# A routed 3x3 convolution whose taps are laid out as half-width matrix products, five pairs of them in place of six full-width ones

## The chip, the cores and the metric

The kernel runs on one core of a Trainium2 chip. Its time is the device time of one launch in microseconds (us), and the time of a kernel is the median of its runs. The engines of the core work side by side and are ordered by semaphores alone: TensorE (PE in the profile; PEld is its weight load), VectorE (DVE), ScalarE (ACT), GpSimd (POOL), and SyncE (SP), which issues most of the DMAs.

## The reference

The input is 32 images of 32x32 pixels and 64 channels, float32. Two stages follow one another, each on a group norm of its input and each added to its input. The first, in which the change lies, is cut to this:

```python
def routed_conv(x, q, Wk, Wv, Wmlp, alpha, We, be):      # x: (32, 32, 32, 64)
    allowed = ones((32, 4))
    for t in range(3):
        k, v = x @ Wk, x @ Wv                             # two heads of 16
        attn = softmax(einsum("nd,bsnd->bns", q, k) / 4)  # over the 1024 pixels
        pooled = einsum("bns,bsnd->bnd", attn, v)
        logits = pooled.reshape(32, 32) @ Wmlp
        weights = softmax(where(allowed, logits, -1e9) / 1.5)
        wsel = weights kept for the two best of four experts, normed to 1
        x_mod = x * (1 + attn.mean(heads) * 1024 * softplus(alpha))
        x = sum_e wsel[:, e] * (conv3x3(x_mod, We[e]) + be[e])
        allowed = allowed without the best expert (the last one stays)
    return x
```

The second stage is two selective state space passes (Mamba), over the rows and over the columns of each image.

## The kernel before

**Layout.** An image lies in 128 partitions by 512 columns: partition 64 r + c holds channel c of the image's rows of parity r (0 the even rows, 1 the odd ones), 16 rows of 32 pixels each. Since a convolution is linear in its weights, the four experts' weights are mixed for each image first, and one 3x3 convolution is made with the mixed weights.

**The convolution.** An output row of one parity needs its own row and the rows above and below it. In this layout three matmuls of 128x128 weights with the padded image `padded` (`pad` in the rows), shifted by the column offset dx = 0, 1, 2, give two of the three row taps for both parities (`conv_main`). What is missing is the tap that lies a whole row pair away: the row above for parity 0, which is a parity 1 row of the pair before, and the row below for parity 1. It takes `shifted` (`shf`), a copy of `padded` moved by one row pair, and three more 128x128 matmuls, of whose weights only the two anti-diagonal 64x64 blocks are not zero (`conv_anti`). Mixed weights `w_mixed` (`wm`) have 2 x 3 x 128 = 768 columns.

**Phases.** The images go in 4 bodies of 8: two groups of 4 (`TEAM`), whose three steps alternate, so that a body has 6 phases, `k` = 0 to 5, and the kernel 24, `P` = 6 i + k. Every engine runs its own written-out program, a `slot` for each phase. In the slot of phase P, the attention and routing of P are worked out, while TensorE makes the convolutions of phase P - 1, which belong to the other group. The order on each engine is that of the code, and is fixed:

- TensorE: `conv_main` of image 0, score of image 3, `conv_anti` of image 0, swap (the largest score over both parities), `conv_main` 1, total (sums of the softmax), `conv_anti` 1, logits, modulation (`p_modul`, the attention map), `conv_main` and `conv_anti` of images 2 and 3, and the scores of images 0 to 2 of the next phase.
- ScalarE: the exponential of the scores (the line that writes `attn_map` from `p_route`; called **the exponential** below), copies of the convolutions' results to `xc`, the exponential of the logits, the map (`attn_map` from `p_modul`), the first product of the mix for the images (`mix`), in some phases the group norm's scaling, and at the end `shift` for the images 0 to 3, which writes `shf`. The next slot begins with the next exponential.
- VectorE: the largest score (`top`), the mixing of weights (three operations for each image, `mix` and `wm`), and the chain of small operations on sums, logits and ranks.
- SyncE stores the map to `map_scratch` and loads it back, spread over the partitions, as `map_all`. GpSimd multiplies `map_all` by `xc` into `pad`, image by image.

So a phase is a ring: the exponential, sums, map, out and back by DMA, `pad`, `shift`, the next exponential. What `shift` waits for stands ahead of it:

```python
        ge(act, conv_done, 4 * (P - 2) + a + 1)
        act.wait_ge(padded_ready, 4 * P + a + 1)
```

Phases differ in what is added. In k = 1 to 4 the results are copied by ScalarE; in k = 5 and 0 VectorE adds the last step's results to the input instead (`step_last`). A group norm is applied in the slots k = 5 and 0 (of the next inputs), and k = 1 and 2 of all bodies but the first (of the outputs). The second stage begins as the last convolutions run, with the first image of the first body.

Of the kernel before, what the change touches and what calls it, by code (L numbers as in the profile page):

```python
# [22 lines left out]
UNITS = IMAGES * 4  # L23
MAIN, ANTI = 3 * 128, 3 * 64
PHASES = 2 * STEPS
# [4 lines left out]
def build(nc, x_in, wk, q, wvT, wmlp, alpha, we, be, mamba_w, out, mid_x, mid_n):  # L30
# [5 lines left out]
    def sb(name, shape, dt=f32):  # L36
        return ctx.enter_context(nc.sbuf_tensor(name, shape, dt))
# [4 lines left out]
    with ctx:  # L42
# [15 lines left out]
        gain = sb("gain", [128, 4])  # L58
        we_sb = sb("we_sb", [128, EXPERTS, 2 * MAIN])
        be_sb = sb("be_sb", [128, EXPERTS])  # L60
# [44 lines left out]

        def anti_of(rows, half, e):
            return we_sb[rows, e, MAIN:].rearrange("p (d c) -> p d c", d=3)[:, :, 64 * half:64 * half + 64]

        first_loads = [(wk_sb[:], wk), (q_sb[:], q.partition_broadcast(128)), (wv_sb[:], wvT), (wmlp_sb[:], wmlp),
                       (gain[:, 0:1], alpha.partition_broadcast(128))]  # L110
        expert_loads = [(be_sb[:], be), (we_sb[:, :, 0:MAIN], we[:, :, 0:MAIN])]
        for par in range(2):
            rows = slice(64 * par, 64 * par + 64)
            for e in range(EXPERTS):
                expert_loads.append((anti_of(rows, 1 - par, e), we[rows, e, MAIN:].rearrange("p (d c) -> p d c", d=3)))
        mamba_loads = []
# [120 lines left out]
        def _(dve):  # L237
# [7 lines left out]
            nc.vector.memset(route[:], 0.0).then_inc(dve_chain, 1)  # L245
            for e in range(EXPERTS):
                for par in range(2):
                    nc.vector.memset(anti_of(slice(64 * par, 64 * par + 64), par, e), 0.0)
            s1["norm_first"](dve)
# [82 lines left out]
def stage1(nc, ctx, memory, x_in, mid_x, norm_rows, c):  # L332
# [6 lines left out]
    R = TEAM * 4 * HEADS * 2  # L339
    ZEROS, ZEROS_DVE = 2 * TEAM * 3, 2 * TEAM * 2 + 2  # L340
    def sb(name, shape, dt=f32):
# [10 lines left out]
    for g in two:  # L352
        xc.append([sb(f"xc_{g}{a}", [128, PIX]) for a in team])
        padded.append([sb(f"pad_{g}{a}", [128, ROWS2, SIDE + 2]) for a in team])
        shifted.append([sb(f"shf_{g}{a}", [128, ROWS2, SIDE + 2]) for a in team])
        w_mixed.append([sb(f"wm_{g}{a}", [128, 2, 3, 128]) for a in team])
        if g == 0:
            mix0 = [sb(f"mix0_{b}", [128, 768]) for b in two]
            map_all = sb("map_all", [128, TEAM, PIX])
            attn_map = sb("attn_map", [128, PIX])  # L360
            attn, map_rows = attn_map[0:R, :], attn_map[R:R + 2 * TEAM, :]
            scrap = sb("scrap", [R, PIX])
            mod_w = sb("mod_w", [R, 128])
    for g in two:
# [177 lines left out]
    def conv_main(pe, i, k, a):  # L542

        g, P = k % 2, i * PHASES + k
        bank = p_conv[a]
        pe.wait_ge(w_ready, 4 * P + a + 1)
        pe.wait_ge(padded_ready, 4 * P + a + 1)

        if k:
            conv_taken(pe, i, k - 1, a)  # L550
        elif i:
            conv_taken(pe, i - 1, PHASES - 1, a)
        elif a == 0:
            pe.wait_ge(c["mamba_ready"], 1)
        for dx in range(3):
            nc.tensor.matmul(bank[:], w_mixed[g][a][:, 0, dx, :], padded[g][a][:, :, dx:dx + SIDE],  # L556
                             start=(dx == 0), stop=False)

    def conv_anti(pe, i, k, a):

        g, P = k % 2, i * PHASES + k
        bank = p_conv[a]
        pe.wait_ge(shifted_ready, 4 * P + a + 1)
        for dx in range(3):
            mm = nc.tensor.matmul(bank[:], w_mixed[g][a][:, 1, dx, :], shifted[g][a][:, :, dx:dx + SIDE],  # L565
                                  start=False, stop=(dx == 2))
        mm.then_inc(conv_done, 1)
# [13 lines left out]
    def tensor_program(pe, prepare):  # L581
        def score(i, k, a):
# [7 lines left out]
            else:  # L590
                pe.wait_ge(x_step, 16 * i + (4 * (k - 2) + a + 1))
            mm = nc.tensor.matmul(p_route[:], route[:, 128 * a:128 * a + 128], xc[g][a][:], start=(a == 0), stop=(a == TEAM - 1))
            if a == TEAM - 1:
# [82 lines left out]
    def shift(act, P, g, a):  # L676

        ge(act, conv_done, 4 * (P - 2) + a + 1)
        act.wait_ge(padded_ready, 4 * P + a + 1)
        nc.scalar.copy(shifted[g][a][0:64, 0:ROWS2 - 1, :], padded[g][a][0:64, 1:, :])  # L680
        nc.scalar.copy(shifted[g][a][64:128, 1:ROWS2, :],  # L681
                       padded[g][a][64:128, :ROWS2 - 1, :]).then_inc(shifted_ready, 1)

# [155 lines left out]
    def mix_last(dve, P, g, a):  # L839
        dve.wait_ge(mix_ready, 8 * P + (3, 4, 7, 8)[a])  # L840

        ge(dve, conv_done, 4 * (P - 2) + a + 1)
        nc.vector.scalar_tensor_tensor(w_mixed[g][a][:].rearrange("p m d c -> p (m d c)"), c["we"][:, 3, :],  # L843
                                       wsel[:, a, 3:4], mix0[a % 2][:], ALU.mult, ALU.add).then_inc(w_ready, 1)

    def norm_first(dve):
# [6 lines left out]
        norm_scale(dve, 0)  # L853
        for g in two:
            for a in team:
                nc.vector.memset(shifted[g][a][0:64, ROWS2 - 1, :], 0.0).then_inc(zeroed_dve, 1)
                nc.vector.memset(shifted[g][a][64:128, 0, :], 0.0).then_inc(zeroed_dve, 1)

# [854 lines left out]
```

## Time and profile before

| | us |
|---|---|
| median of 3 runs | 3948.51 (3946.25 to 3951.95) |
| profiled execution, its own time | 3952.92 |
| its span in the trace | 3951.1 |
| first exponential of the first stage | at 27.5 |
| 24th exponential | at 644.1 |
| VectorE busy over the span | 3750.3 (95%) |
| TensorE | 3655.9 (93%) |
| GpSimd | 3278.0 (83%) |
| ScalarE | 2937.1 (74%) |

The busy shares are over the whole span, five sixths of which is the second stage. What bounds the first stage is read from its own stretch and from the order of the instructions in one phase. A matmul on float32 data stands in the trace as two instructions, one for each of two passes, so that "x6" is three matmuls of the code.

### The profile page before, as it was taken

What the parts mean: (1) busy time and instruction counts of PE and PEld (TensorE: products, weight loads), DVE (VectorE), ACT (ScalarE), POOL (GpSimd) and SP (SyncE); (2) the same over time, 40 slices, a digit from 0 to 9 for tenths busy, and PEclk for the clock granted to TensorE, in tenths of its full rate; (3) what the DMA queues carried; (4) which work ended last, traced back from release to release, by engine and by line L of the source; (5) the groups of instructions that cost most, each with busy time, mean ns of one, the idle gap of its engine ahead of it and who ended that gap; (6) DMA issues with size and microseconds to landing.
All of it is one profiled execution on the core that took longest, in us unless ns stands there. A gap on an engine that the chain in (4) does not pass through costs nothing. (4 is left out here: it accounts for less than half of the span.)

```text
span 3951.1 us, 34661 instructions
## 1 busy us (share of the span) xinstructions
PE 3655.9 (93%) x8780; PEld 1520.5 (38%) x8780; DVE 3750.3 (95%) x3409; ACT 2937.1 (74%) x4422; POOL 3278.0 (83%) x1542
## 2 busy tenths in 40 slices
PE   7999999899999999999999999999999999999998
PEld 3444444333333333333333333333333333333333
DVE  7778787999999999999999999999999999999998
ACT  3454554788777788888888878888888888887785
POOL 2221222899999999999999999999999999999998
PEclk9999999999999999999999999999999999999999
DMA  4142324888889888988889988899888898998886
GB/s 113 33 130 57 108 73 151 322 341 341 340 344 353 344 342 348 349 346 338 347 347 344 352 352 345 343 351 347 347 339 346 346 346 347 352 351 340 343 345 254
DMA packets 203159, 1181.08 MB, mean 299 GB/s; under 512 B 30960, under 2 KB 31760, under 8 KB 68816
## 3 DMA queue, kind: packets, MB, share of 16 engines
q1 hardware_dynamic: 200128, 1177.64, 78.3%
q10 hardware_dynamic: 2832, 1.23, 0.1%
q8 instruction: 70, 1.15, 0.1%
q14 instruction: 129, 1.06, 0.1%
HBM read 1144.03 MB, written 34.73 MB: 298 GB/s over the span
## 5 line engine op out<-in xcount | busy, mean ns | idle before, releaser
L1547 POOL TENSOR_TENSOR read<-state,bc_all 128x1024 f32<-128x1024 f32 x1024 | 2399.4, 2360 | 127.6 <-DVE state L1611 97.7
L1611 DVE TENSOR_TENSOR_SCAN state<-decays,p_drive 128x1024 f32<-128x1024 f32 x1024 | 2297.8, 2274 | 35.2 <-ACT p_drive L1446 12.2
L1316 PE MATMUL p_y<-read,ident 128*128 128x512 f32 x4096 | 1920.5, 602 | 12.8 <-POOL read L1547 12.8
L1438 ACT ACTIVATE decays<-dt,wa 128x496 f32<-128x496 f32 x2048 | 1337.1, 703 | 122.1 <-DVE state L1611 119.7
L1316 PEld LDWEIGHTS p_y<-read,ident 128*128 128x128 f32 x4096 | 766.2, 191 | 987.6 <-issue 841.8
L1598 DVE TENSOR_TENSOR p_drive<-bc_all,p_dtx 128x1024 f32<-128x1024 f32 x768 | 906.3, 1210 | 0.0
L1564 POOL TENSOR_TENSOR pool_drive<-dtx,bc_all 128x1024 f32<-128x1024 f32 x256 | 602.4, 2353 | 4.4 <-DMA bc_all<-bc_scratch 4.2
L766 POOL TENSOR_TENSOR pad<-map_all,xc 128x512 f32<-128x512 f32 x96 | 139.5, 1483 | 519.1 <-DMA map_all<-map_scratch 455.3
L1446 ACT COPY p_drive<-pool_drive 128x1024 f32<-128x1024 f32 x256 | 260.8, 1019 | 271.5 <-DVE state L1611 271.5
L1312 PE MATMUL p_y<-xconv,d_diag 128*128 128x512 f32 x256 | 145.1, 649 | 204.2 <-DVE gated L1621 204.2
L556 PE MATMUL p_conv<-pad,wm 128*128 128x512 f32 x576 | 267.6, 600 | 1.2 <-issue 0.8
L565 PE MATMUL p_conv<-shf,wm 128*128 128x512 f32 x576 | 265.5, 597 | 1.3 <-ACT shf L681 1.3
L1554 POOL TENSOR_TENSOR dtx<-dt,xconv 128x512 f32<-128x512 f32 x128 | 163.6, 1278 | 12.0 <-ACT dt L1410 12.0
L705 ACT ACTIVATE mix<-we_sb,wsel 128x768 f32<-128x768 f32 x96 | 87.1, 933 | 116.2 <-DVE wm L843 72.4
L1292 PE MATMUL p_b<-soft,ident 128*128 128x512 f32 x256 | 144.4, 646 | 30.0 <-ACT soft L1431 30.0
L1394 ACT ACTIVATE gate<-p_b 128x512 f32<-128x512 f32 x128 | 76.4, 597 | 120.7 <-PE p_b L1269 66.2
L1387 ACT ACT_TABLE_LOAD x128 | 164.2, 1283 | 2.3
L1398 ACT ACT_TABLE_LOAD x128 | 164.2, 1283 | 2.3
L1312 PEld LDWEIGHTS p_y<-xconv,d_diag 128*128 128x128 f32 x256 | 38.3, 188 | 310.3 <-DVE gated L1621 309.3
L556 PEld LDWEIGHTS p_conv<-pad,wm 128*128 128x128 f32 x576 | 104.8, 189 | 136.2 <-issue 115.3
L565 PEld LDWEIGHTS p_conv<-shf,wm 128*128 128x128 f32 x576 | 106.6, 189 | 130.0 <-issue 122.9
L1255 PE MATMUL p_a<-cols_in,w_cols 128*128 128x256 f32 x640 | 148.8, 378 | 1.0 <-issue 0.5
(162 smaller groups left out, 3215.7 us busy)
## 6 DMA issues: line engine op xcount, KB each, us to landing
bc_all<-bc_scratch SPq DMA_DIRECT2D x1024, 1024.0 KB, 7.2
map_all<-map_scratch SPq DMA_DIRECT2D x48, 512.0 KB, 5.7
norm_rows<-xn SPq DMA_DIRECT2D x32, 280.0 KB, 5.6
norm_in<-norm_rows SPq DMA_DIRECT2D x64, 140.0 KB, 8.1
norm_in<-norm_rows SPq DMA_DIRECT2D x64, 139.8 KB, 8.3
fresh<-in_x SPq DMA_DIRECT2D x32, 256.0 KB, 6.6
x<-in_x SPq DMA_DIRECT2D x32, 256.0 KB, 3.5
mid_x<-x SPq DMA_DIRECT2D x32, 256.0 KB, 6.5
```

Of the source, the lines that this page charges most:

```text
L556: nc.tensor.matmul(bank[:], w_mixed[g][a][:, 0, dx, :], padded[g][a][:, :, dx:dx + SIDE], start=(dx == 0), stop=False)
L565: mm = nc.tensor.matmul(bank[:], w_mixed[g][a][:, 1, dx, :], shifted[g][a][:, :, dx:dx + SIDE], start=False, stop=(dx == 2))
L1312: nc.tensor.matmul(p_y[:], d_diag[unit[0]][:], xconv[b][:], start=True, stop=False).then_inc(skip_added, 1)
L1316: nc.tensor.matmul(p_y[:], ident[:], read[:, s % DEEP, :], start=False, stop=(s == N - 1)).then_inc(y_added, 1)
L1387: nc.scalar.activation(same_shape(xconv[b][:], m), in_order(p_a, m), ACT.Silu, bias=wcb[m][:]).then_inc(xconv_ready, 1)
L1398: nc.scalar.preload_act_table_set("natural_log_exp_and_others")
L1438: nc.scalar.activation(decays[:, s % DEEP, :].rearrange("p (q t) -> p q t", t=SIDE)[:, :, 1:], dt[b][:, :, 1:], ACT.Exp, scale=wa[m][:, s: ...
L1446: nc.scalar.copy(p_drive[:, s % 4:s % 4 + 2, :], pool_drive[n][:]).then_inc(drive_moved, 1)
L1547: nc.gpsimd.tensor_tensor(read[:, s % DEEP:s % DEEP + 2, :], state[:, s % DEEP:s % DEEP + 2, :], bc_all[s // CHUNK][:, :, 1, :], ALU.mult) ...
L1564: nc.gpsimd.tensor_tensor(pool_drive[n][:], dtx[b][:].unsqueeze(1).broadcast_to([128, 2, PIX]), bc_all[s // CHUNK][:, :, 0, :], ALU.mult). ...
L1598: nc.vector.tensor_tensor(p_drive[:, 2 * (p % 2):2 * (p % 2) + 2, :], bc_all[p][:, :, 0, :], p_dtx[:].unsqueeze(1).broadcast_to([128, 2, P ...
L1611: nc.vector.tensor_tensor_scan(state[:, at:at + 2, :].rearrange("p s n -> p (s n)"), decays[:, at:at + 2, :].rearrange("p s n -> p (s n)") ...
```

## The change

The two anti-diagonal blocks of `conv_anti` are not put into a 128x128 matrix with zeros. Each parity's output gets products of its own, with 64 columns of weights (all 128 partitions of input), and writes its own half of the bank's partitions. `conv_main` is three pairs of such products. For the taps that are missing, three of 64 channels for each parity, two of them share one product's 128 partitions of input and the third has one for itself, so that `conv_anti` is two pairs. Each parity therefore has a `shifted` buffer of its own, which holds the missing rows twice: once as they were, and once, in the other 64 partitions, one column further. `shift` makes four copies an image in place of two. The `shifted` buffers are no longer doubled over the two groups, so that `shift` waits for the convolution of the phase before (`P - 1`) and not for the one before that. Mixed weights have 384 + 256 = 640 columns in place of 768. The scores are split into two half-width products as well. Expert loads, zeroed regions and the placing of buffers follow.

```diff
-MAIN, ANTI = 3 * 128, 3 * 64
+MAIN, ANTI = 3 * 128, 4 * 64
+MIX = MAIN + ANTI
...
         for dx in range(3):
-            nc.tensor.matmul(bank[:], w_mixed[g][a][:, 0, dx, :], padded[g][a][:, :, dx:dx + SIDE],
-                             start=(dx == 0), stop=False)
+            for par in two:
+                nc.tensor.matmul(bank[CH * par:CH * par + CH, :],
+                                 w_mixed[g][a][:, 128 * dx + CH * par:128 * dx + CH * par + CH],
+                                 padded[g][a][:, :, dx:dx + SIDE], start=(dx == 0), stop=False)
...
-        for dx in range(3):
-            mm = nc.tensor.matmul(bank[:], w_mixed[g][a][:, 1, dx, :], shifted[g][a][:, :, dx:dx + SIDE],
-                                  start=False, stop=(dx == 2))
+        for n in two:
+            for par in two:
+                at = MAIN + 128 * par + CH * n
+                mm = nc.tensor.matmul(bank[CH * par:CH * par + CH, :], w_mixed[g][a][:, at:at + CH],
+                                      shifted[par][a][:, :, 1 + n:1 + n + SIDE], start=False, stop=(n == 1))
...
-            mm = nc.tensor.matmul(p_route[:], route[:, 128 * a:128 * a + 128], xc[g][a][:], start=(a == 0), stop=(a == TEAM - 1))
+            for part in two:
+                mm = nc.tensor.matmul(p_route[R * part:R * part + R, :], route[:, 128 * a + R * part:128 * a + R * part + R],
+                                      xc[g][a][:], start=(a == 0), stop=(a == TEAM - 1))
...
-        ge(act, conv_done, 4 * (P - 2) + a + 1)
+        ge(act, conv_done, 4 * (P - 1) + a + 1)
         act.wait_ge(padded_ready, 4 * P + a + 1)
-        nc.scalar.copy(shifted[g][a][0:64, 0:ROWS2 - 1, :], padded[g][a][0:64, 1:, :])
-        nc.scalar.copy(shifted[g][a][64:128, 1:ROWS2, :],
-                       padded[g][a][64:128, :ROWS2 - 1, :]).then_inc(shifted_ready, 1)
+        for par, source, there, here in ((0, slice(64, 128), slice(1, ROWS2), slice(0, ROWS2 - 1)),
+                                         (1, slice(0, 64), slice(0, ROWS2 - 1), slice(1, ROWS2))):
+            crossed = slice(64 * par, 64 * par + 64)
+            nc.scalar.copy(shifted[par][a][source, there, 1:], padded[g][a][source, here, 1:])
+            o = nc.scalar.copy(shifted[par][a][crossed, there, 1:], padded[g][a][source, here, :SIDE + 1])
+        o.then_inc(shifted_ready, 1)
...
-        nc.vector.scalar_tensor_tensor(w_mixed[g][a][:].rearrange("p m d c -> p (m d c)"), c["we"][:, 3, :],
+        nc.vector.scalar_tensor_tensor(w_mixed[g][a][:], c["we"][:, 3, :],
                                        wsel[:, a, 3:4], mix0[a % 2][:], ALU.mult, ALU.add).then_inc(w_ready, 1)
```

On ScalarE, between the last results of one phase and the map of the next, there stood before (`xc` is the result of image 3, then come the copies of the four images, then the next slot's exponential):

```order
L698 ACTIVATE xc<-p_conv,bias 128x512
L680 COPY shf<-pad 64x510
L681 COPY shf<-pad 64x510
L680 COPY shf<-pad 64x510
L681 COPY shf<-pad 64x510
L680 COPY shf<-pad 64x510
L681 COPY shf<-pad 64x510
L680 COPY shf<-pad 64x510
L681 COPY shf<-pad 64x510
L714 ACTIVATE attn_map,parts<-p_route,neg_top 64x512
L698 ACTIVATE xc<-p_conv,bias 128x512
L721 ACTIVATE prob<-logit 128x16
```

Now sixteen copies stand in that place; these are the last two images' eight and what follows:

```order
L698 COPY shf<-pad 64x15x33
L699 COPY shf<-pad 64x15x33
L698 COPY shf<-pad 64x15x33
L699 COPY shf<-pad 64x15x33
L698 COPY shf<-pad 64x15x33
L699 COPY shf<-pad 64x15x33
L698 COPY shf<-pad 64x15x33
L699 COPY shf<-pad 64x15x33
L732 ACTIVATE attn_map,parts<-p_route,neg_top 64x512
L716 ACTIVATE xc<-p_conv,bias 128x512
L739 ACTIVATE prob<-logit 128x16
```

The exponential stands behind eight more copies than before, and each copy is of 495 elements in 15 pieces instead of 510 in one.

On TensorE a phase read as follows before, from its first convolution to the modulation and the next convolutions:

```order
L556 MATMUL p_conv<-pad,wm 128x512 x3
L592 MATMUL p_route<-xc,route 128x512
L565 MATMUL p_conv<-shf,wm 128x512 x3
L598 MATMUL p_small<-top,neg_swap 128x1
L556 MATMUL p_conv<-pad,wm 128x512 x3
L602 MATMUL p_small<-parts,both_par 128x2
L565 MATMUL p_conv<-shf,wm 128x512 x3
L606 MATMUL p_small<-ratios,ones 128x16
L612 MATMUL p_modul<-attn_map,mod_w 128x512
L556 MATMUL p_conv<-pad,wm 128x512 x3
L565 MATMUL p_conv<-shf,wm 128x512 x3
```

Now the same place reads:

```order
L566 MATMUL p_conv<-pad,wm 64x512 x6
L606 MATMUL p_route<-xc,route 64x512 x2
L578 MATMUL p_conv<-shf,wm 64x512 x4
L613 MATMUL p_small<-top,neg_swap 128x1
L566 MATMUL p_conv<-pad,wm 64x512 x6
L617 MATMUL p_small<-parts,both_par 128x2
L578 MATMUL p_conv<-shf,wm 64x512 x4
L621 MATMUL p_small<-ratios,ones 128x16
L627 MATMUL p_modul<-attn_map,mod_w 128x512
L566 MATMUL p_conv<-pad,wm 64x512 x6
L578 MATMUL p_conv<-shf,wm 64x512 x4
```

Here 64x512 is the size of a product's result. The order is the same; a full-width product of the convolution or the score has become a pair, and `conv_anti` has two pairs for three products. Three times in a phase a full-width product (swap; total; logits and modulation) stands between half-width ones.

## Rows read from the trace of the kernel before

**Rows 1.** Busy time by engine in a stretch of the first stage.

```profile
core 0: us, PE busy (x) PEld busy (x) DVE busy (x) ACT busy (x) POOL busy (x), PEclk, DMA share, GB/s
...
400.00:500.00 100.00, 100.00 (x254) 44.80 (x253) 75.22 (x203) 50.00 (x83) 16.31 (x14) 1.00 0.38 108
```

**Rows 2.** The exponential's line, all of its executions.

```profile
L714 ACT ACTIVATE attn_map<-p_route,neg_top x24: 682/682/682, 27.5 to 644.1; 64x512 f32<-64x512 f32 x24
```

**Rows 3.** Order of time (start us, us, what, count, [idle before <-releaser]): ScalarE, phase 15.

```profile
430.70 0.68 ACT L714 ACTIVATE attn_map<-p_route,neg_top 64x512 f32<-64x512 f32 x1 [1.73 <-DVE neg_top L916]
...
438.66 0.58 ACT L726 ACTIVATE attn_map<-p_modul 8x512 f32<-8x512 f32 x1
...
449.55 0.62 ACT L680 COPY shf<-pad 64x510 f32<-64x510 f32 x1 [0.39 <-POOL pad L766]
...
453.98 0.61 ACT L681 COPY shf<-pad 64x510 f32<-64x510 f32 x1
456.76 0.68 ACT L714 ACTIVATE attn_map<-p_route,neg_top 64x512 f32<-64x512 f32 x1 [2.17 <-DVE neg_top L916]
```

**Rows 4.** VectorE in order of time, phase 15: between exponential and map.

```profile
432.24 1.94 DVE L836 SCALAR_TENSOR_TENSOR mix<-we_sb,wsel,mix 128x768 f32<-128x768 f32 x2
...
435.89 0.28 DVE L946 TENSOR_SCALAR mod_w<-spread,kmap 64x128 f32<-64x128 f32 x1
436.09 1.00 DVE L843 SCALAR_TENSOR_TENSOR wm<-we_sb,wsel,mix 128x768 f32<-128x768 f32 x1
```

**Rows 5.** TensorE in order of time, phase 15: image 2, image 0 of the next slot.

```profile
437.28 2.84 PE L556 MATMUL p_conv<-pad,wm 128*128 128x512 f32 x6
...
450.26 2.74 PE L556 MATMUL p_conv<-pad,wm 128*128 128x512 f32 x6
```

**Rows 6.** GpSimd in order of time, phase 15: the four images' `pad`.

```profile
448.20 4.95 POOL L766 TENSOR_TENSOR pad<-map_all,xc 128x512 f32<-128x512 f32 x4 [20.85 <-DMA map_all<-map_scratch]
```

**Rows 7.** ScalarE in order of time, phase 14 (k = 2): exponential, first copy.

```profile
404.30 0.68 ACT L714 ACTIVATE attn_map<-p_route,neg_top 64x512 f32<-64x512 f32 x1 [1.63 <-DVE neg_top L916]
...
423.94 0.60 ACT L680 COPY shf<-pad 64x510 f32<-64x510 f32 x1
```

**Rows 8.** ScalarE in order of time, phase 5 (k = 5): exponential, first copy, next exponential.

```profile
159.28 0.68 ACT L714 ACTIVATE attn_map<-p_route,neg_top 64x512 f32<-64x512 f32 x1 [2.63 <-DVE neg_top L916]
...
181.44 0.60 ACT L680 COPY shf<-pad 64x510 f32<-64x510 f32 x1
...
187.50 0.68 ACT L714 ACTIVATE attn_map<-p_route,neg_top 64x512 f32<-64x512 f32 x1 [1.03 <-DVE neg_top L916]
```

**Rows 9.** VectorE in order of time, phase 5: last mix operations and step_last beside GpSimd.

```profile
176.60 3.97 DVE L843 SCALAR_TENSOR_TENSOR wm<-we_sb,wsel,mix 128x768 f32<-128x768 f32 x2
180.49 1.40 DVE L822 SCALAR_TENSOR_TENSOR x<-p_conv,bias,x 128x512 f32<-128x512 f32 x2
```

**Rows 10.** ScalarE, second stage: a 496-element operation in pieces.

```profile
685.73 2.50 ACT L1438 ACTIVATE decays<-dt,wa 128x496 f32<-128x496 f32 x4
```

**Rows 11.** TensorE, second stage: two half-width float32 products (x4), and their first two starts.

```profile
2059.43 0.67 PE L1335 MATMUL p_a<-gated,wo 128*64 128x256 f32 x4
...
2059.43 0.45 PE L1335 MATMUL p_a<-gated,wo 128*64 128x256 f32 x2
```

**Rows 12.** TensorE, second stage: one half-width product between full-width ones.

```profile
2006.82 1.45 PE L1316 MATMUL p_y<-read,ident 128*128 128x512 f32 x3
2008.20 1.07 PE L1325 MATMUL p_a<-gated,wo 128*64 128x512 f32 x2
2009.20 1.12 PE L1316 MATMUL p_y<-read,ident 128*128 128x512 f32 x2
```

**Rows 13.** Windows around a fall of TensorE's clock, second stage.

```profile
930.00:938.60 8.60, 6.46 (x15) 2.49 (x14) 8.60 (x7) 7.54 (x14) 7.97 (x5) 1.00 1.01 424
938.60:942.10 3.50, 3.50 (x5) 1.35 (x4) 3.41 (x3) 1.65 (x3) 3.42 (x2) 0.51 1.03 405
```

**Rows 14.** TensorE in order of time just before that fall.

```profile
938.22 1.72 PE L1312 MATMUL p_y<-xconv,d_diag 128*128 128x512 f32 x2 [1.90 <-DVE gated L1621]
```

**Rows 15.** VectorE: the last result of the first stage.

```profile
689.92 0.75 DVE L822 SCALAR_TENSOR_TENSOR x<-p_conv,bias,x 128x512 f32<-128x512 f32 x1 [2.17 <-PE p_conv L565]
```

More of the change, by code:

```diff
@@ L58, in build @@
         gain = sb("gain", [128, 4])
-        we_sb = sb("we_sb", [128, EXPERTS, 2 * MAIN])
+        we_sb = sb("we_sb", [128, EXPERTS, MIX])
         be_sb = sb("be_sb", [128, EXPERTS])
@@ L104, in build, with anti_of, tap_of @@
         dve_chain = sem("dve_chain")
-        def anti_of(rows, half, e):
-            return we_sb[rows, e, MAIN:].rearrange("p (d c) -> p d c", d=3)[:, :, 64 * half:64 * half + 64]
+        low, high = slice(0, 64), slice(64, 128)
+        def anti_of(rows, out_par, n):
+            at = MAIN + 128 * out_par + 64 * n
+            return we_sb[rows, :, at:at + 64]
+        def tap_of(rows, dx):
+            return we[rows, :, MAIN + 64 * dx:MAIN + 64 * dx + 64]
         first_loads = [(wk_sb[:], wk), (q_sb[:], q.partition_broadcast(128)), (wv_sb[:], wvT), (wmlp_sb[:], wmlp),
@@ L111, in build @@
         expert_loads = [(be_sb[:], be), (we_sb[:, :, 0:MAIN], we[:, :, 0:MAIN])]
[L112 to L115, printed above, removed]
+        for out_par, straight, crossed in ((0, high, low), (1, low, high)):
+            expert_loads += [(anti_of(straight, out_par, 0), tap_of(straight, 1)), (anti_of(straight, out_par, 1), tap_of(straight, 2)),
+                             (anti_of(crossed, out_par, 0), tap_of(straight, 0))]
         mamba_loads = []
@@ L245, in _ @@
             nc.vector.memset(route[:], 0.0).then_inc(dve_chain, 1)
-            for e in range(EXPERTS):
-                for par in range(2):
-                    nc.vector.memset(anti_of(slice(64 * par, 64 * par + 64), par, e), 0.0)
+            nc.vector.memset(anti_of(low, 0, 1), 0.0)
+            nc.vector.memset(anti_of(high, 1, 1), 0.0)
             s1["norm_first"](dve)
@@ L339, in stage1 @@
     R = TEAM * 4 * HEADS * 2
-    ZEROS, ZEROS_DVE = 2 * TEAM * 3, 2 * TEAM * 2 + 2
+    ZEROS, ZEROS_DVE = 2 * TEAM * 3, 2 * TEAM + 2
     def sb(name, shape, dt=f32):
@@ L354, in stage1 @@
         padded.append([sb(f"pad_{g}{a}", [128, ROWS2, SIDE + 2]) for a in team])
-        shifted.append([sb(f"shf_{g}{a}", [128, ROWS2, SIDE + 2]) for a in team])
-        w_mixed.append([sb(f"wm_{g}{a}", [128, 2, 3, 128]) for a in team])
+        w_mixed.append([sb(f"wm_{g}{a}", [128, MIX]) for a in team])
         if g == 0:
-            mix0 = [sb(f"mix0_{b}", [128, 768]) for b in two]
+            mix0 = [sb(f"mix0_{b}", [128, MIX]) for b in two]
+            scrap = sb("scrap", [R, PIX])
+            mod_w = sb("mod_w", [R, 128])
+            sb("spare", [128, 1760])
+            shf_00 = sb("shf_00", [128, ROWS2, SIDE + 2])
             map_all = sb("map_all", [128, TEAM, PIX])
@@ L361, in stage1 @@
             attn, map_rows = attn_map[0:R, :], attn_map[R:R + 2 * TEAM, :]
-            scrap = sb("scrap", [R, PIX])
-            mod_w = sb("mod_w", [R, 128])
+    for par in two:
+        shifted.append([shf_00 if a == par == 0 else sb(f"shf_{par}{a}", [128, ROWS2, SIDE + 2]) for a in team])
     for g in two:
@@ L563, in conv_anti @@
         pe.wait_ge(shifted_ready, 4 * P + a + 1)
-        for dx in range(3):
-            mm = nc.tensor.matmul(bank[:], w_mixed[g][a][:, 1, dx, :], shifted[g][a][:, :, dx:dx + SIDE],
-                                  start=False, stop=(dx == 2))
+        for n in two:
+            for par in two:
+                at = MAIN + 128 * par + CH * n
+                mm = nc.tensor.matmul(bank[CH * par:CH * par + CH, :], w_mixed[g][a][:, at:at + CH],
+                                      shifted[par][a][:, :, 1 + n:1 + n + SIDE], start=False, stop=(n == 1))
         mm.then_inc(conv_done, 1)
@@ L853, in norm_first @@
         norm_scale(dve, 0)
[L854 to L857, printed above, removed]
+        for a in team:
+            nc.vector.memset(shifted[0][a][:, 0, :], 0.0).then_inc(zeroed_dve, 1)
+            nc.vector.memset(shifted[1][a][:, ROWS2 - 1, :], 0.0).then_inc(zeroed_dve, 1)
     def last_vector(dve, part):
```

## The prediction

> **What bounds the kernel now.** I read the busy time by stretch first. In the first stage TensorE is busy all the time, the others half to three quarters [rows 1]. That suggests that fewer matmuls make it faster. But a phase is a ring, and one must see how close behind TensorE the ring's other parts are. So next I read one phase in order of time on each engine. The exponential is the best mark, since it comes once a phase: 24 of them from 27.5 to 644.1 us [rows 2], 26.8 us apart on average.
>
> In phase 15 they are 26.06 us apart [rows 3]. From the exponential to the first copy of `shift` pass 18.85 us: sums, `mod_w`, map, DMA out and back, `pad`. The eight copies start 0.633 us apart (7 steps from 449.55 to 453.98) and end at 454.59, 5.04 us after they began. Then ScalarE idles 2.17 us for `neg_top`, which hangs on TensorE [rows 3]. That 2.17 us is all the room the copies have. On TensorE, image 0 of the next slot starts at 450.26 [rows 5], 0.8 us after its `pad` is there (448.20 + 4.95/4 = 449.44) [rows 6]. So TensorE leads, but the ring through ScalarE and the DMAs is only 0.8 us (`pad`) and 2.2 us (`shift`) behind. Once TensorE is shortened by more than that, the ring decides.
>
> The 23 intervals between exponentials are of three kinds, counted in the same view. Eleven are as in phase 15 (ten at 26.1; the first one, with the preparations, 27.5). Six are as in phase 14, with a norm of outputs (26.3 to 26.4): 19.64 us to the first copy, then 6.76 [rows 3, 7]. Six are as in phase 5 (28.2; one is 29.3): 22.16 us to the first copy, then 6.06, and there the exponential already follows the end of the copies (181.44 + 5.03 = 186.47) by 1.03 us [rows 8]. Together 10 x 26.1 + 27.5 + 6 x 26.35 + 5 x 28.2 + 29.3 = 617, the 616.6 of [rows 2].
>
> **The change, part by part.**
>
> *TensorE's products.* From 437.28 to 450.26 stand 15 full products, four times three of the convolution and three scores: 0.865 us each, two passes of 0.43 [rows 5]. Do two half-width products run side by side? The second stage has such a pair, on 256 columns. Two passes end within 0.45 us, all four within 0.67 [rows 11], so the second pair of passes ends 0.22 after the first, where a lone pass of 256 columns would need 0.43/2 = 0.215. They run together, and a pair costs what one full product does: 0.43 to 0.44 a pass. Saved: 4 images x (6 - 5) = 4 products, 3.4 us a phase; the scores' pairs cost nothing.
>
> *Changing between full and half width.* In the second stage three full passes from 2006.82 would be followed at 2006.82 + 3 x 0.43 = 2008.11; the half-width product starts at 2008.20 (+0.09), holds the engine 1.00 in place of 0.86 (+0.14), and the next full product's two passes take 1.12 in place of the usual 1.02 (+0.10) [rows 12]. That is 0.34 us there and back, three times a phase: 1.0 us. TensorE's own need is then 26.06 - 3.4 + 1.0 = 23.7 us a phase.
>
> The Trainium skill has this in TensorEngine Tiling, Key Properties: a change of tiling mode drains the engine, while tiles of one mode work independently. The trace agrees with both, at 0.34 us and 0.22 us. By that page's table of theoretical speedup alone one would book the 3.4 us a phase and stop; that is the rival "hidden" below.
>
> *VectorE's mixing.* At 768 columns two operations take 1.94 us, one 1.00 [rows 4], a spacing of 0.94. At 512 columns two take 1.40 and one 0.75 [rows 9, 15], 0.65. For 640 I take 0.80, a gain of 0.14 each (bounds 0 and 0.16, the full proportion). Four stand between exponential and map: two `mix` at 432.24, one `wm` before `mod_w`, one before the logits that the map's line on ScalarE is queued behind [rows 3, 4]. The ring gains 0.55 us. In phases like 5 the first copy waits for ScalarE's last mix, which waits for `wm`. There four more `mix` (0.55), two `wm` that beside GpSimd take 1.99 each and should scale to 1.66 (0.65) [rows 9], and ScalarE's part (0.1) are won: 1.8 in all.
>
> *The copies.* Sixteen in place of eight, all ahead of the next exponential in ScalarE's queue. No row shows a copy of 64x15x33, or one from one half of the partitions to the other. Nearest above is the present copy, 0.633 for 510 elements [rows 3]. Nearest in size and in pieces are four operations of 496 elements in 2.50, under 0.625 each [rows 10]. Below, the map's line with 8 partitions still takes 0.58 [rows 3], so fewer partitions don't make it cheap. I take 0.61, with 0.58 and 0.66 as ends (the latter if pieces and crossing add 8% of the present copy). Sixteen take 9.8 us from first start to the exponential.
>
> *The new wait on the convolution of the phase before* costs nothing: image 3 of it is through before TensorE begins image 0 of the next slot, and that is after `pad` [rows 5, 6]. Loads, memsets and placement touch the start alone; I take zero.
>
> **The sum.** The new distance from first copy to next exponential is 9.8 us wherever the copies decide. `neg_top` comes earlier: TensorE needs, from `pad`, 3 + 1 + 2 pairs (5.2 us), swap and one change of width, about 6 us.
> - Like phase 15: 9.78 in place of 7.21 is +2.57, less 0.55: +2.0, eleven times, 22.2.
> - Like phase 14: 9.78 for 6.76 is +3.02, less 0.55, and less 0.2 since the first copy now follows `pad` directly (0.1 as in phase 15, not 0.3): +2.3, six times, 13.6.
> - Like phase 5: 9.78 for 6.06 is +3.72, less 1.8: +1.9, six times, 11.5.
>
> That is 47.3 us up to the 24th exponential. From there to the last result at 689.9 [rows 15] TensorE has 4 products fewer and a few more changes of width, and ScalarE has eight more copies among the second stage's first steps; they roughly cancel, +0.5. The second stage is untouched. 48 us on the profiled execution's own 3952.9 is 4001; the median before is 4.4 lower, so **3997**.
>
> Is TensorE really behind the ring then? From 437.28 to 450.26 it will have 13 pairs for 15 products: 11.2 us for 12.98, so image 0 waits some 0.7 us for `pad` (which moves little against `mod_w`). At total it has, from `pad`, 9 pairs, swap and changes, 8.2 us; the sums come at 0.1 + 9.8 + 1.5 (430.70 to 432.24) = 11.4 [rows 3, 4]. It idles 3.3 us there, every phase.
>
> **Rivals.**
>
> *The clock falls and TensorE leads again.* In the second stage, after an idle of 1.90 us, the granted clock is 0.51 for 3.5 us: the 1.2 GHz level [rows 13, 14]. A 3.3 us idle each phase invites it. Such a stretch costs up to 1.7 us of matmul time; about 1.0 us of it would fall into TensorE's wait for `mod_w` and 0.7 into the wait for `pad`, so one fall a phase costs nearly nothing, and two up to 1.7 x 23 = 39. I take +20 as this case: 4017. Dearer passes do the same: from 0.457 us a pass (13 pairs, 0.7 us of room) each 0.01 costs 0.26 a phase, 6 us in all. The skill's TensorE: Matmul & The Clock Gate, on HAM oscillation, warns of just such gaps between bursts; rows 13 show it here, and by the page alone one would expect it in each phase.
>
> *Halves do not overlap* in a long row of pairs, so the change doesn't do what its name says. Then 48 half products at 0.86, 2 and 1 us make 44.3 a phase: +18.2 x 24 = 437, 4385. Against it: rows 11, one pair long.
>
> *Faster: the copies stay hidden.* If the exponential did not wait for them, a phase like 15 would take 18.85 - 0.55 + about 5.9 = 24.2, near TensorE's 23.7: -1.9 x 24 = -45, 3904. It decides at a copy's spacing of (7.21 + 0.55)/16 = 0.48 us; every row of ScalarE at this size is at 0.58 or more.
>
> **Chances.** The sum as worked out 0.72, its own range 3984 to 4014 (copies -11 and +18 us, the rest +-3). Clock or passes 0.15. No overlap 0.03. Hidden 0.04. Cases between that and the sum 0.06, half of them within 0.2%, which is about what a measurement of this kernel can tell from no change. So faster 0.04, same 0.03, slower 0.93. The range of 8 in 10 reaches down a little below the sum's own and well into the clock's case: 3980 to 4030.
>
> **What would show it.** In the profile after: exponentials about 28 us apart in phases like 15, 28.6 like 14, 30 like 5; sixteen copies 0.61 apart ending right at the exponential, with ScalarE's idle before it gone; TensorE idle some 3 us before total, released by VectorE's sums, and no longer at full busy share; pairs of passes 0.43 apart with starts together. The prediction is wrong if the exponential does not follow the last copy, if copies cost under 0.5 or over 0.7, or if the granted clock of the first stage lies well under 0.9.

## The result, and the profile after

The changed kernel takes 4005.04 us (median of four, 4001.16 to 4008.35) against 3950.23 for the kernel before: a ratio of 1.0134, 95% interval 1.0115 to 1.0152. It is slower by 53 us going by the ratio, by 54.8 going by the two medians; the forecast was 3997, slower by 48. The profiled execution below is the fastest of the four, 4001.16 us on its own clock, 48.2 more than the profiled one before.

The exponential's line, all executions:

```profile
L732 ACT ACTIVATE attn_map<-p_route,neg_top x24: 682/682/683, 26.8 to 694.0; 64x512 f32<-64x512 f32 x24
```

From the first to the 24th pass 667.2 us, where it was 616.6 [rows 2]: 50.6 of the difference lies there. What comes after the 24th takes 3305.0 us of the span of 3999.0, before 3307.0. That is 2 us less, and the same part of the experiments' profiles differs by as much among themselves (3305.9 in the first, 3310.1 in the fifth below), so it says nothing.

ScalarE in phase 15, in order of time (start us, us, what, count, idle before and its releaser); between the shown copies stand fourteen more:

```profile
465.10 0.68 ACT L732 ACTIVATE attn_map<-p_route,neg_top 64x512 f32<-64x512 f32 x1
...
472.53 0.58 ACT L744 ACTIVATE attn_map<-p_modul 8x512 f32<-8x512 f32 x1
...
482.90 0.60 ACT L698 COPY shf<-pad 64x495 f32<-64x495 f32 x1 [0.87 <-POOL pad L784]
...
492.17 0.60 ACT L699 COPY shf<-pad 64x495 f32<-64x495 f32 x1
492.79 0.68 ACT L732 ACTIVATE attn_map<-p_route,neg_top 64x512 f32<-64x512 f32 x1
```

Set beside [rows 3], all three steps are there. The copies start (492.17 - 482.90)/15 = 0.618 us apart. The exponential begins 0.62 after the last one starts, and the idle time in brackets is gone: it waits for nothing but its queue. From first copy to exponential pass 9.89 us in place of 7.21. From exponential to map pass 7.43 in place of 7.96, the shorter mixing. No copy of the whole run waits for TensorE: where L698 has idle time before it (11 times, 8.5 us in all), `pad` ends it, and L699 never has any.

TensorE in the same phase:

```profile
462.40 2.80 PE L566 MATMUL p_conv<-pad,wm 128*64 128x512 f32 x12
466.78 0.38 PE L617 MATMUL p_small<-parts,both_par 128*128 128x2 f32 x2 [1.58 <-DVE parts L947]
467.09 1.94 PE L578 MATMUL p_conv<-shf,wm 128*64 128x512 f32 x8
...
470.23 1.12 PE L627 MATMUL p_modul<-attn_map,mod_w 64*128 64x512 f32 x2 [0.84 <-DVE mod_w L963]
```

Six half-width products, twelve passes, stand within 2.80 us, where three full ones take 2.84 us [rows 5]: pairs run side by side in a long row as well. And TensorE now waits twice, for the sums and for `mod_w`. The busy shares of a stretch show the same. TensorE has gone from 100.00 [rows 1] to 87.52, and the granted clock from 1.00 to 0.91:

```profile
core 0: us, PE busy (x) PEld busy (x) DVE busy (x) ACT busy (x) POOL busy (x), PEclk, DMA share, GB/s
400.00:500.00 100.00, 87.52 (x358) 29.55 (x358) 63.06 (x191) 65.82 (x113) 14.93 (x12) 0.91 0.35 108
```

Phase 2 shows what the clock does; its exponentials are 29.2 us apart, in phase 15 they are 27.7. First windows, then TensorE in order of time:

```profile
80.00:85.40 5.40, 3.04 (x15) 1.00 (x14) 0.92 (x4) 5.28 (x11) 0.00 (x0) 1.00 0.00 0
85.40:95.70 10.30, 9.51 (x22) 3.19 (x24) 8.28 (x30) 2.67 (x6) 0.00 (x0) 0.50 0.01 3
95.70:100.00 4.30, 4.30 (x22) 1.39 (x20) 4.19 (x6) 1.50 (x4) 0.00 (x0) 1.00 0.92 198
```

```profile
86.19 0.58 PE L617 MATMUL p_small<-parts,both_par 128*128 128x2 f32 x2 [3.15 <-DVE parts L947]
86.71 3.68 PE L578 MATMUL p_conv<-shf,wm 128*64 128x512 f32 x8
...
90.77 2.05 PE L627 MATMUL p_modul<-attn_map,mod_w 64*128 64x512 f32 x2
```

TensorE idles 3.15 us before the total, and 2.4 us into this the granted clock falls to 0.50, its 1.2 GHz level, for 10.2 us. The four products of `conv_anti` take 3.68 us for 1.94, and the modulation, which waited for `mod_w` in phase 15, now has no idle time before it: it is late by TensorE itself. ScalarE in the same phase, whose exponential is at 84.52, then waits for TensorE twice:

```profile
92.85 0.58 ACT L744 ACTIVATE attn_map<-p_modul 8x512 f32<-8x512 f32 x1 [0.27 <-PE p_modul L627]
...
103.05 0.69 ACT L716 ACTIVATE xc<-p_conv,bias 128x512 f32<-128x512 f32 x1 [1.50 <-PE p_conv L578]
103.82 0.60 ACT L698 COPY shf<-pad 64x495 f32<-64x495 f32 x1
```

The map comes 8.33 us after the exponential, in phase 15 7.43, and the first copy 19.30 us after it, in phase 15 17.80. That is the 1.5 us between the two phases, most of it the clock's (the fifth experiment has 27.88 us for phase 2).

The clock doesn't fall in every phase, nor always for as long. Of the 22 phases from 1 to 22, seven have a fall of 10.2 us, one of 6.8, nine of 3.4, and five (8, 11, 15, 20 and 22) have none; each of these five comes right behind one with a fall of 6.8 or 10.2, and TensorE idles only 1.2 to 1.6 us before the total there. The idle time alone does not tell, though: phase 3 has 1.63 us and a fall of 3.4, phase 15 has 1.58 and none. The phases like 15 with a fall of 10.2 (2, 10 and 21) take 29.2 to 29.4 us, the seven others 27.6 to 28.3.

The Trainium skill's TensorE: Matmul & The Clock Gate, on HAM oscillation, tells of waits between bursts of matmuls that send the clock back to half each time. The trace agrees on the fall (0.50 in the window above), but here it comes in 17 of the 22 phases.

A phase with a norm of inputs, 11, on ScalarE:

```profile
345.63 0.68 ACT L732 ACTIVATE attn_map<-p_route,neg_top 64x512 f32<-64x512 f32 x1
...
366.47 0.60 ACT L698 COPY shf<-pad 64x495 f32<-64x495 f32 x1
...
376.37 0.68 ACT L732 ACTIVATE attn_map<-p_route,neg_top 64x512 f32<-64x512 f32 x1
```

Here too the exponential follows sixteen copies at once, 9.90 us after the first; 20.84 us lie ahead of them, where phase 5 had 22.16 [rows 8]. The last result of the first stage, on VectorE, comes 46.0 us after the 24th exponential, before 45.8 [rows 2, 15]:

```profile
739.96 0.75 DVE L840 SCALAR_TENSOR_TENSOR x<-p_conv,bias,x 128x512 f32<-128x512 f32 x1 [1.36 <-PE p_conv L578]
```

### The profile page after: what moved, and what is told of

It reads as the page before. It is cut to its first block and busy times, and to the rows that moved or that the text cites. A ratio compares the mean times of both kernels' runs of the same rounds, so it can differ in the third digit from the quotient of the medians.

```text
span 3999.0 us, 36761 instructions
## 1 busy us (share of the span) xinstructions
PE 3632.1 (91%) x9740; PEld 1447.0 (36%) x9740; DVE 3704.4 (93%) x3395; ACT 3042.4 (76%) x4614; POOL 3267.3 (82%) x1542
## 3 DMA queue, kind: packets, MB, share of 16 engines
q8 instruction: 78, 1.28, 0.1%
## 5 line engine op out<-in xcount | busy, mean ns | idle before, releaser
L784 POOL TENSOR_TENSOR pad<-map_all,xc 128x512 f32<-128x512 f32 x96 | 128.2, 1368 | 578.7 <-DMA map_all<-map_scratch 578.7
L566 PE MATMUL p_conv<-pad,wm 128*64 128x512 f32 x1152 | 278.6, 620 | 3.1 <-issue 3.1
L578 PE MATMUL p_conv<-shf,wm 128*64 128x512 f32 x768 | 210.1, 673 | 1.7 <-ACT shf L699 1.7
L566 PEld LDWEIGHTS p_conv<-pad,wm 128*64 128x64 f32 x1152 | 81.7, 141 | 175.8 <-issue 170.4
L1302 PE MATMUL p_b<-xconv,wdt 128*128 128x512 f32 x256 | 144.8, 647 | 0.0
L723 ACT ACTIVATE mix<-we_sb,wsel 128x640 f32<-128x640 f32 x96 | 76.4, 826 | 85.8 <-DVE wm L861 45.0
```

What stands on the lines that cost most here:

```text
L566: nc.tensor.matmul(bank[CH * par:CH * par + CH, :], w_mixed[g][a][:, 128 * dx + CH * par:128 * dx + CH * par + CH], padded[g][a][:, :, dx: ...
L578: mm = nc.tensor.matmul(bank[CH * par:CH * par + CH, :], w_mixed[g][a][:, at:at + CH], shifted[par][a][:, :, 1 + n:1 + n + SIDE], start=Fa ...
```

## The experiments

The theory: sixteen copies stand in the ring ahead of the exponential, and their 9.9 us are longer than what TensorE gained. The rivals: TensorE itself became slower (passes, changes of width), or the clock did it. Each ratio is against runs of the kernel before on the same chip.

**e1_exp_first: the copies of images 2 and 3 behind the exponential.**

```diff
             if steps:
                 step_out(i, k - 1, 0)
+            if P:
+                shift(act, P - 1, 1 - g, 2)
+                shift(act, P - 1, 1 - g, 3)
             if norm:
                 group_root(act, norm[0])
...
             shift(act, P, g, 1)
-            if after:
-                shift(act, P, g, 2)
-                shift(act, P, g, 3)
```

> The changed kernel, but ScalarE makes the copies of images 2 and 3 behind the next phase's exponential (and behind its first result) and not ahead of it; the same sixteen copies. Theory of the prediction (the copies stand in the ring ahead of the exponential): 8 copies or 4.9 us are left there, the exponential waits for neg_top again, the interval of phases like 15 falls from 28 to 24.3, of those like 14 to 24.7, of those like 5 to 26.5, and the whole to 3912 (3900 to 3925), faster than both kernels. Rival (TensorE's passes, changes of width or fallen clock are what made it slower): the order on ScalarE changes little, 3990 to 4005.

3906.71 us, ratio 0.9884 (0.9867 to 0.9900). One execution of the four took 14853.61 us; it is left out of the ratio, and nothing in the profile, which is of another execution, says why. The same sixteen copies and the same products are now 43 us faster than the kernel before and 98 faster than the changed one. All that moved is where eight copies stand. In phase 16 on ScalarE:

```profile
425.39 0.68 ACT L732 ACTIVATE attn_map<-p_route,neg_top 64x512 f32<-64x512 f32 x1 [1.15 <-DVE neg_top L933]
...
426.76 0.60 ACT L698 COPY shf<-pad 64x495 f32<-64x495 f32 x1
...
431.09 0.60 ACT L699 COPY shf<-pad 64x495 f32<-64x495 f32 x1
432.00 0.22 ACT L742 ACTIVATE prob<-logit 128x16 f32<-128x16 f32 x1 [0.30 <-DVE logit L975]
...
443.38 0.60 ACT L698 COPY shf<-pad 64x495 f32<-64x495 f32 x1 [1.07 <-POOL pad L784]
...
449.45 0.68 ACT L732 ACTIVATE attn_map<-p_route,neg_top 64x512 f32<-64x512 f32 x1 [1.15 <-DVE neg_top L933]
```

The exponential waits for `neg_top` again, as in [rows 3], and the eight copies end 0.3 us before the logits come: they fit into a gap that ScalarE has anyway. The interval is 24.06 us. TensorE is not the bound there either: it idles 0.44 us before image 0 of the next slot and starts it at 443.39, when `pad` has also released the first copy (443.38).

```profile
440.20 2.75 PE L606 MATMUL p_route<-xc,route 128*64 128x512 f32 x12
443.39 2.80 PE L566 MATMUL p_conv<-pad,wm 128*64 128x512 f32 x12 [0.44 <-issue]
```

**e2_before_16_copies: the kernel before, with the copies made twice.**

```diff
...
+        ge(act, copied, 2 * (4 * P + a))
+        nc.scalar.copy(extra[0:64, 0:ROWS2 - 1, :], padded[g][a][0:64, 1:, :]).then_inc(copied, 1)
+        nc.scalar.copy(extra[64:128, 1:ROWS2, :], padded[g][a][64:128, :ROWS2 - 1, :]).then_inc(copied, 1)
         nc.scalar.copy(shifted[g][a][0:64, 0:ROWS2 - 1, :], padded[g][a][0:64, 1:, :])
```

> The kernel before with its full-width products, but each image's shift makes its two copies a second time, into a buffer that nobody reads: sixteen copies a phase. Theory: the ring becomes exp to first copy plus 16 x 0.633 us, that is 29.0, 29.6 and 32.3 us for the three kinds of phase, and the whole 3950 + 76 = 4026 (4015 to 4040), slower than the changed kernel, which has the shorter mixing. Rival (copies hidden, products at fault): 3950.

4039.69 us, ratio 1.0231 (1.0214 to 1.0249). Full-width products and all, more copies alone make it slower by 90 us. The forecast was 76, and 4039.69 is at the end of its range. The ring's last part works as forecast in phase 15 (`extra` is in bfloat16, so its copies are casts, no dearer):

```profile
485.18 0.68 ACT L719 ACTIVATE attn_map<-p_route,neg_top 64x512 f32<-64x512 f32 x1
...
506.00 0.62 ACT L683 CAST extra<-pad 64x510 bf16<-64x510 f32 x1 [0.45 <-POOL pad L771]
...
515.54 0.61 ACT L686 COPY shf<-pad 64x510 f32<-64x510 f32 x1
516.18 0.68 ACT L719 ACTIVATE attn_map<-p_route,neg_top 64x512 f32<-64x512 f32 x1
```

First copy to exponential is 10.18 us, forecast 10.13 (16 x 0.633). But the first copy comes 20.82 us after the exponential, where 18.85 was taken, and the phase takes 31.0 us. The clock is at work here too, on TensorE:

```profile
486.85 0.59 PE L604 MATMUL p_small<-parts,both_par 128*128 128x2 f32 x2 [2.71 <-DVE parts L935]
487.29 5.47 PE L567 MATMUL p_conv<-shf,wm 128*128 128x512 f32 x6
```

TensorE waits 2.71 us for the sums and is granted 0.50 for 6.8 us from 486.5 on; `conv_anti` takes 5.47 us, in the kernel before 2.82, and the map comes 9.80 us after the exponential for 7.96. So phase 15 is the dearest of its kind. The five phases of the kind that have no fall (1, 3, 10, 16 and 22) take 28.5 to 29.0 us, where 29.0 was forecast. Over the first 22 intervals the map comes 10.4 us later in all than in the kernel before, and every phase in which it is late by more than 0.1 us has a fall: most of the 14 us that the forecast lacked is the clock.

**e3_before_pairs: the kernel before, every product of convolution and scores as a pair.**

```diff
-            nc.tensor.matmul(bank[:], w_mixed[g][a][:, 0, dx, :], padded[g][a][:, :, dx:dx + SIDE],
-                             start=(dx == 0), stop=False)
+            for par in two:
+                nc.tensor.matmul(bank[CH * par:CH * par + CH, :], w_mixed[g][a][:, 0, dx, CH * par:CH * par + CH],
+                                 padded[g][a][:, :, dx:dx + SIDE], start=(dx == 0), stop=False)
```

(The anti-diagonal products and the scores likewise.)

> The kernel before, with each full-width product of the convolution and of the scores made as a pair of half-width ones (the zero blocks too), so six pairs an image; nothing else changed. Theory: pairs cost what full products do, and three changes of width there and back cost 1.0 us a phase where TensorE leads (17 phases), so 3950 + 17 = 3967 (3955 to 3975). Rival (halves overlap badly in a long row): each 10% on a pass is 24 us more; without any overlap about 4400.

3956.84 us, ratio 1.0015 (1.0005 to 1.0024), so +6 us where +17 was forecast. The swap's product comes once a phase; in phases 15 and 16 on TensorE:

```profile
460.07 0.38 PE L602 MATMUL p_small<-top,neg_swap 128*128 128x1 f32 x2
460.39 2.80 PE L557 MATMUL p_conv<-pad,wm 128*64 128x512 f32 x12
...
486.46 0.38 PE L602 MATMUL p_small<-top,neg_swap 128*128 128x1 f32 x2
```

26.39 us for a phase that took 26.06. Six pairs cost what six full products cost, and three changes of width there and back cost 0.33 us, not 1.0. TensorE has no idle time at any of the three places, so none of the price is hidden in a wait. The swap shows a part of it: `conv_main` starts 0.32 us after it, in the kernel before 0.14, and behind the total it is the same. The third place, logits and modulation together, takes 1.28 us from first start to the next convolution, before 1.39, though the modulation has 512 columns like the product of [rows 12]. Why that one cost 0.34 and this one nothing is not shown.

**e4_after_8_copies: the changed kernel without the crossed copies.** It leaves out part of the convolution: where a crossed copy would have stood, the products read zeros, written at the start by memsets that the cut below does not show.

```diff
-            nc.scalar.copy(shifted[par][a][source, there, 1:], padded[g][a][source, here, 1:])
-            o = nc.scalar.copy(shifted[par][a][crossed, there, 1:], padded[g][a][source, here, :SIDE + 1])
+            o = nc.scalar.copy(shifted[par][a][source, there, 1:], padded[g][a][source, here, 1:])
```

> The changed kernel without the crossed copies: shift makes two copies an image. It leaves out part of the computation: the missing row's third tap in the packed products reads zeros, written once at the start (about 2.5 us more there). Theory: as with the copies behind the exponential, 3914 (3900 to 3925), TensorE leads with 23.7 to 24.3 us a phase. Rival (not the copies): 3990 to 4005.

3913.23 us, ratio 0.9907 (0.9892 to 0.9921), the forecast being 3914. ScalarE in phase 15, the eight copies in one row and the exponential after them:

```profile
448.43 4.96 ACT L698 COPY shf<-pad 64x495 f32<-64x495 f32 x8 [1.12 <-POOL pad L783]
454.51 0.68 ACT L731 ACTIVATE attn_map<-p_route,neg_top 64x512 f32<-64x512 f32 x1 [1.12 <-DVE neg_top L934]
```

The exponential comes 6.08 us after the first copy, released by `neg_top`, the same distance as in e1 (443.38 to 449.45). Removing eight copies and moving eight copies give the same ring.

**e5_after_filled: TensorE's idle time before total filled.**

```diff
+                pe.wait_ge(neg_top_ready, P + 1)
+                for _ in range(3):
+                    nc.tensor.matmul(p_small[:, 64:512], c["both_par"][:], padded[1 - k % 2][1][:, :, 1:29],
+                                     start=True, stop=True)
...
             total(P)
```

> The changed kernel, with three full-width products of 448 columns that nobody reads put into TensorE's idle time before total, about 2.3 us of the 3.1 it waits there for the sums. They leave the ring as it is. Theory: the changed kernel's long intervals (29.2 to 29.6 us where the rest of their kind is at 28.0) come from stretches at 1.2 GHz that its idle time brings on; with the idle time filled, the granted clock goes from 0.98 to 0.99, phases like 15 take 27.7 to 28.1 throughout, and the whole is 8 us less than the changed kernel's 4005: 3997 (3990 to 4001). Rival (the clock's stretches are covered by TensorE's waits, the long intervals have another cause): 4003 to 4008, or more if the products are in the way.

3998.53 us, ratio 1.0113 (1.0098 to 1.0128), where the changed kernel had 1.0134: 6.5 us less by the medians, 8 by the ratios. The two intervals overlap, so the times alone would leave it open. The profile does not. A later stretch, phase 2 again, and TensorE in it:

```profile
400.00:500.00 100.00, 92.23 (x392) 32.71 (x392) 64.27 (x193) 63.80 (x109) 14.93 (x12) 1.00 0.38 115
80.00:110.00 30.00, 28.14 (x122) 9.63 (x118) 15.99 (x46) 18.76 (x33) 4.97 (x4) 1.00 0.16 36
```

```profile
82.40 2.64 PE L646 MATMUL p_small<-pad,both_par 128*128 128x448 f32 x6
85.62 0.38 PE L617 MATMUL p_small<-parts,both_par 128*128 128x2 f32 x2 [0.58 <-DVE parts L951]
85.93 1.94 PE L578 MATMUL p_conv<-shf,wm 128*64 128x512 f32 x8
```

With 0.58 us idle in place of 3.15 the clock stays at 1.00, `conv_anti` takes 1.94 us again, and all ten phases of this kind lie at 27.6 to 28.1 us (four of them at 28.3 to 29.4 in the changed kernel). Over the whole stretch from 50 us to the 24th exponential the granted clock is 1.00, in the changed kernel 0.92. From first to 24th exponential pass 661.0 us for 667.2, one execution each. More work on TensorE makes the kernel faster, by 6 to 8 us. The rest, 44.4 us over the kernel before, is what the copies cost, less what the shorter mixing gives back.

**e6_before_exp_first: e1's order in the kernel before.** The same edit as in e1.

> The kernel before, with the same order on ScalarE as in e1_exp_first: copies of images 2 and 3 behind the next exponential. Theory: TensorE leads there and the copies end before neg_top in every phase, so nothing changes: 3950 (3944 to 3953). Rival (the order itself is what e1 gained by): about 3860 to 3900.

3951.70 us, ratio 0.9995 (0.9986 to 1.0005): no change, as forecast. The order gives nothing as long as TensorE leads. So e1's gain is that of the changed products, five pairs and the shorter mixing that goes with them, once the exponential no longer waits for its queue.

**e7_map_first: the ring shortened further.**

```diff
-            late(mix_last, 2)
             chain(dve, nc.vector.tensor_scalar(kmap[:], r[:], float(PIX), c["gain"][0:R, 3:4], ALU.mult, ALU.mult))
             ge(dve, modul_done, P)
             nc.vector.tensor_scalar(mod_w[:], c["spread"][:], kmap[:], None, ALU.mult).then_inc(mod_w_ready, 1)
+            late(mix_last, 2)
```

and on ScalarE the map's three lines stand ahead of those that write `prob`.

> As e1_exp_first, and the ring shortened once more: VectorE makes mod_w ahead of the mix's last operation for image 2, and ScalarE makes the map ahead of the exponential of the logits. Theory: in e1 the ring leads by 0.4 us in every phase but those like 5 (TensorE waits for pad). The map comes 1.1 us sooner, TensorE's own need of about 23.4 us decides, 0.7 us less in 17 phases: 3894 (3888 to 3900). Rival (TensorE waits for the weights of image 2 instead, now mixed later): 3905.

3907.89 us, ratio 0.9887 (0.9873 to 0.9902): nothing over e1, where 3894 was forecast. The time is near the rival's 3905, but in phases like 15 not for its reason. The interval of phases like 15 did fall, to 23.00 us (forecast 23.4), and TensorE has no idle time in it any more:

```profile
426.08 0.68 ACT L732 ACTIVATE attn_map<-p_route,neg_top 64x512 f32<-64x512 f32 x1 [1.02 <-DVE neg_top L933]
...
449.08 0.68 ACT L732 ACTIVATE attn_map<-p_route,neg_top 64x512 f32<-64x512 f32 x1 [0.92 <-DVE neg_top L933]
```

Over the ten phases of the kind that is 10.6 us less than in e1. The others took it back: the six like 5 rose by 5.6 us in all, the six like 14 by 2.5 and the first by 1.7. Phase 5 rose from 26.59 to 27.96. VectorE, then GpSimd, in e7:

```profile
161.80 2.69 DVE L854 SCALAR_TENSOR_TENSOR mix<-we_sb,wsel,mix 128x640 f32<-128x640 f32 x2
164.41 3.71 DVE L861 SCALAR_TENSOR_TENSOR wm<-we_sb,wsel,mix 128x640 f32<-128x640 f32 x2
```

```profile
162.19 7.07 POOL L784 TENSOR_TENSOR pad<-map_all,xc 128x512 f32<-128x512 f32 x4 [17.82 <-DMA map_all<-map_scratch]
```

The sooner map lets `pad` run beside more of the mixing, and both slow down: the two mix operations take 2.69 us, in e1 1.67, and the four `pad` 7.07, in e1 6.45, and 4.97 in e1's phase 4, where no mixing runs beside them. The mixing ends 1.37 us later after the exponential than in e1, as much as the interval rose, and about 1.0 of it is that pair of operations. There the copies wait for the mixing, not for `pad`, so sooner was worse. What lengthened the phases like 14 and the first one is open.

**e8_map_first_plain: the sooner map in the ten phases like 15 alone.** The edit of e7 under `if 1 <= k <= PHASES - 2 and not norm`, the order of e1 otherwise.

> As e7_map_first, but the sooner map only in the ten phases like 15 (k = 1 to 4 without a norm); the others keep the order of e1_exp_first. In e7 those ten went from 24.1 to 23.0 us, but phases like 5 went from 26.6 to 27.9, since pad then ran beside VectorE's mixing (two mix operations 2.69 us and GpSimd's four 7.07, in place of 1.67 and 6.45), and those like 14 from 24.4 to 24.9. Theory: the gain stays and the loss goes, 10 x 1.1 us under e1: 3896 (3891 to 3901). Rival (what the ten phases gain is lost elsewhere, or was not tied to them): 3904 to 3909.

3897.06 us, ratio 0.9860 (0.9844 to 0.9876); forecast 3896. The exponential's line:

```profile
L732 ACT ACTIVATE attn_map<-p_route,neg_top x24: 682/682/684, 25.7 to 585.9; 64x512 f32<-64x512 f32 x24
```

560.2 us from first to 24th, for 573.7 in e1. It is the fastest version here, 56 us under the kernel before and 108 under the changed one.

## Why the prediction was right, point by point

**What bounds, and what would next.** Right: TensorE led by 0.8 and 2.2 us only, and the ring took over. e2 (copies alone: +90 us, some 10 of it through the clock) and e1 and e4 (copies moved or gone: -43 and -36 against the kernel before) show it from both sides, e6 shows that order alone does nothing.

**Pairs cost what full products do.** Right: [rows 11], one pair long, held for rows of six, 2.80 us for 2.84, and for the whole kernel in e3.

**Changes of width, 1.0 us a phase.** Wrong in size: 0.33 in e3. The price of one place in the second stage was taken three times, for swap, total, and logits with modulation, two of which cost 0.18 us each and the third nothing. It did not enter the sum, since the ring leads, but TensorE's own need was put at 23.7 us and is 23.0 (e7): 26.06 - 3.4 + 0.33.

**Copies at 0.61 us, sixteen ahead of the exponential.** Right: 0.618, in 15 pieces and over the halves; 9.89 us against 9.8.

**The wait on the convolution of the phase before.** Right at nothing: no copy waits for TensorE.

**The sum up to the 24th exponential, 47.3 us.** 44.4 in e5, where the clock stays up. By kinds of phase, all in e5: the ten like 15 +1.8 us each for +2.0 and the first interval +2.5; the six like 14 +1.7 for +2.3; the six like 5 +2.2 for +1.9. The errors go both ways. In phases like 5 two `wm` beside GpSimd take 3.71 us, not 3.3: shorter operations under contention did not scale in full. In phases like 14 the forecast had the wrong link. It let `pad` release the first copy and took the 0.3 us behind it in phase 14 for all six, but in the other five the first copy of the kernel before comes 0.8 to 1.0 us after `pad`. It hangs on the mixing there, as in phases like 5; ScalarE just before the first copy of [rows 7]:

```profile
421.60 1.86 ACT L705 ACTIVATE mix<-we_sb,wsel 128x768 f32<-128x768 f32 x2 [1.14 <-DVE wm L843]
423.37 0.67 ACT L698 ACTIVATE xc<-p_conv,bias 128x512 f32<-128x512 f32 x1
```

ScalarE waits for VectorE's `wm`, and from there to the copy at 423.94 it has no idle time. More of the phase's mixing stands ahead of that than ahead of the map, so more of the shortening counts: the first copy comes 18.1 us after the exponential in e5, before 19.64, 1.5 us sooner and not 0.75.

**The clock.** Put at almost nothing in the sum, with the two waits of 1.0 and 0.7 us as cover. That holds for the falls of 3.4 us: the five phases like 15 that have one take 28.06 us on average, the same five in e5 27.95. The falls of 10.2 us are longer than TensorE's waits can cover. Both together cost 667.2 - 661.0 = 6.2 us in the profiled executions, by the ratios 8. It is the rival "the clock falls" in small, next to the main case and not in its place. TensorE's idle time before the total was forecast at 3.3 us in every phase; it is 1.2 to 3.8, least where the phase before had a long fall (phase 15: 1.58).

**The number.** That it came so near is partly luck. Up to the 24th exponential 47.3 us were forecast and 50.6 measured, which are 44.4 for the ring and 6.2 for the clock: the ring was put 2.9 us too high, the clock about 6 too low.

**The tail and the second stage.** +0.2 us to the stage's last result, forecast +0.5; the rest cannot be told from run to run.

## What to carry to other kernels

An engine that is busy all the time may lead a ring by less than a microsecond: before taking work off it, measure how late each other link of the ring would be, and count what the change puts into the queues of those links. Where the new work is not needed soon, let it stand behind the link that others wait for; moving eight copies was worth 98 us here, against the changed kernel. And a cheaper order in one kind of phase can be a dearer one in another, so orders that are written by hand are best chosen for each kind.

## What the runs showed of the hardware

- Two half-width float32 products of 512 columns in alternating halves share one pass time, 0.43 us, in rows of six pairs: twelve passes in 2.80 us.
- Full-width products between half-width ones cost 0.33 us a phase for three such places (e3): 0.18 each for products of 1 and 2 columns, nothing for logits and modulation (16 and 512 columns).
- A copy of 495 elements in 15 pieces, from one half of the partitions to the other too, is no dearer than one of 510 in a piece: 0.618 us against 0.633.
- Where TensorE idled 1.2 to 3.8 us once a phase, its clock went to the 1.2 GHz level in 17 of 22 phases, for 3.4, 6.8 or 10.2 us at a time. Filling the idle time with useless products, down to 0.2 to 1.2 us, kept it at 2.4 GHz and gave back 6 to 8 us.
- VectorE and GpSimd slow each other: two operations of 128x640 on VectorE take 1.67 us alone and up to 3.71 beside GpSimd's `pad`, and four `pad` go from 4.97 to as much as 7.07 (e1, e7).
